# A top-1 expert layer computed densely, against one that first sorts the rows by expert through DRAM and then computes 88 tiles of one expert each

## What is computed

```python
router_logits = xf @ Wr + br                      # [10000, 8]
topk_logits, topk_idx = jax.lax.top_k(router_logits, TOP_K)      # TOP_K = 1
topk_gates = jax.nn.softmax(topk_logits, axis=1)
for k in range(TOP_K):
    idx_k = topk_idx[:, k]
    gate_k = topk_gates[:, k:k + 1]
    for e in range(E):                            # E = 8
        h = jax.nn.relu(xf @ W1[e] + b1[e])       # 512 -> 64
        oe = h @ W2[e] + b2[e]                    # 64 -> 512
        mask = (idx_k == e)[:, None]
        out = out + jnp.where(mask, gate_k * oe, 0.0)
...
x = x + _L0_ffn_ref(_layernorm(x, axis=-1)[None], ...)[0]
```

## Time and profile before

| | us |
|---|---|
| median of 3 runs | 2736.06 (2735.32 to 2736.74) |
| the profiled execution | 2733.61 |
| its span in the trace | 2731.8 |
| `nodes`, first PE work to the wait before `hidden` | about 10 to 1010 |
| `hidden` | about 1018 to 1487 |
| `mix` | about 1487 to 2132 |
| `ffn` | 2132 to 2732 |

### The profile page before, as it was taken

One profiled execution on the slowest core, in us unless ns is written; L12 is line 12 of the kernel. 1 busy time (PEld: TensorE's weight loads), 2 busy tenths in 40 slices (PEclk: granted clock), 3 DMA queues, 4 the chain that ended last, 5 costly groups with the idle time before them and its releaser, 6 DMA issues.

```text
span 2731.8 us, 36032 instructions
## 1 busy us (share of the span) xinstructions
PE 2612.9 (96%) x11712; PEld 2081.5 (76%) x11712; DVE 1836.8 (67%) x3708; ACT 1031.0 (38%) x1805; POOL 1061.6 (39%) x1009
## 2 busy tenths in 40 slices
PE   5999999999999989999999788999999899999999
PEld 4788888888888868888886556677777677777777
DVE  5577777777778744444443677788886677777774
ACT  3455454444444434443443232233332132232232
POOL 5677766666666620000000455555554111111110
PEclk9999999999999999999999899999999999999999
DMA  9767665555555554444444478787887332232231
GB/s 367 246 174 201 174 194 145 146 139 135 145 125 157 126 156 180 189 172 185 185 185 162 147 192 224 217 241 220 233 227 179 145 139 93 94 137 93 105 125 46
DMA packets 134566, 460.66 MB, mean 169 GB/s; under 512 B 26649, under 2 KB 27161, under 8 KB 99137
## 3 DMA queue, kind: packets, MB, share of 16 engines
q1 hardware_dynamic: 98624, 375.21, 37.6%
q0 software_dynamic: 35840, 84.23, 17.0%
HBM read 240.62 MB, written 218.76 MB: 168 GB/s over the span
## 4 chain that ended last, share of the span: by engine, by line
PE 82%; DMA 7%; DVE 5%; SPq 2%; issue 2%; ACT 2%; POOL 1%; POOLq 0%; DVEq 0%; ACTq 0%
PE bank L1206 63%; PE bank L1257 8%; DMA agg_d<-O,eidx 5%; PE bank L1213 3%; PE bank L1321 2%; DVE x2T_low L314 2%; PE bank L1421 1%; PE bank L417 1%; PE bank L418 1%; SPq L484 1%; DVE f_relu L1125 1%; PE bank L1332 1%; ACT f_relu L884 1%; SPq L486 1%; PE bank L1406 1%
## 5 line engine op out<-in xcount | busy, mean ns | idle before, releaser
L378 POOL DMA_INDIRECT agg_d<-O,eidx x160 | 275.4, 1721 | 234.6 <-DMA agg_d<-O,eidx 165.7
L314 POOL TENSOR_TENSOR G_low<-G,G_high 128x512 fp32r<-128x512 f32 x160 | 244.0, 1525 | 209.0 <-ACT G_high L439 209.0
L361 POOL DMA_INDIRECT G<-y_d,esrc x80 | 87.2, 1090 | 529.8 <-DMA y_d<-b_y 516.9
L397 DVE SCALAR_TENSOR_TENSOR Sj<-erow,dstf,tri 128x128 f32<-128x128 int32 x160 | 188.7, 1179 | 55.4 <-DMA agg_d<-O,eidx 55.3
L720 POOL TENSOR_SCALAR veps<-mv 128x1 f32<-128x1 f32 x80 | 26.5, 332 | 487.2 <-DVE mv L1098 487.2
L439 ACT CAST G_high<-G 128x512 fp32r<-128x512 f32 x160 | 99.2, 620 | 198.5 <-DVE G L958 175.4
L406 DVE SCALAR_TENSOR_TENSOR eidx<-cnt,todump,dstf 128x1 int32<-128x1 f32 x160 | 139.7, 873 | 7.6
L685 POOL TENSOR_TENSOR pd<-pd,low 128x512 f32<-128x512 f32 (+1 forms) x80 | 143.2, 1790 | 0.0
L314 POOL TENSOR_TENSOR a_xn_rows_low<-a_x,a_xn_rows_high 128x512 fp32r<-128x512 f32 x80 | 142.7, 1783 | 0.2 <-ACT a_xn_rows_high L749 0.2
L850 ACT CAST qz_high<-low 128x512 fp32r<-128x512 f32 x80 | 49.6, 620 | 239.4 <-PE bank L1206 152.5
L1206 PE MATMUL bank<-Wk_high,xnT_high 128*128 128x512 f32 x320 | 127.9, 400 | 6.3 <-DVE xnT_low L314 6.3
...
## 6 DMA issues: line engine op xcount, KB each, us to landing
...
q_d<-q_rows SPq DMA_DIRECT2D x80, 256.0 KB, 2.4
r_d<-r_rows SPq DMA_DIRECT2D x80, 256.0 KB, 3.8
...
```

The source lines that it names most:

```text
L314: return eng.tensor_tensor(out_, full, high.bitcast(F32), ALU.subtract)
L361: pool.indirect_dma_start(G[:, j, :], None, table, bass.IndirectOffsetOnAxis(ap=esrc[:, b, j:j + 1], axis=0)).then_inc(e_g[j], 16)
L378: pool.indirect_dma_start(agg, bass.IndirectOffsetOnAxis(ap=eidx[:, j, 0:1], axis=0), O[:, j, 0:width], None, compute_op=ALU.add).then_inc ...
L397: dve.scalar_tensor_tensor(Sj[:, :], row, dstf[:, b, j:j + 1], tri[:, :], ALU.is_equal, ALU.mult, accum_out=cnt[:, j:j + 1]).then_inc(e_cn ...
```

## The change

`nodes`, the fold, `hidden` and `mix` stay as they are, but for semaphores that are merged and for preparations of the last stage: POOL's clearing at t = 10 of `mix` goes away, two copies on ACT and two subtractions on DVE go away, and SP loads other constants (a table of 573 KB, later the weights' halves). In their place `ffn` becomes two passes with a hinge between them.

**`route`**, 20 groups: x2 and its statistics as before, now into `rows` with 8 extra words for each row (mean, 1/sqrt, -mean/sqrt, gate, row number). ACT makes the normalised rows, PE turns them, ACT evacuates them unsplit, and PE computes the logits by fp32 matmuls with 8 moving columns (4 for each tile), row form. DVE finds the maximum and the one-hot without an index instruction; PE ranks the rows inside the group by matmuls with a lower-triangular and an all-ones matrix (8 matmuls), DVE adds the running count of each expert, and POOL scatters the rows (2080 bytes each) to their place in `xs_d`, an area for each expert.

**The hinge**: DVE computes from the eight counts, by 19 instructions each waiting for the one before, two tables of 88 entries: the expert of a tile and its first row. SP writes a padding tile of 128 rows behind the last row of each expert (8 DMAs at an address read from SBUF into a register) and waits for the scatters.

**`expert`**, 88 tiles of 128 rows of one expert (80 full tiles, and at most one broken tile for each expert): SP reads the tile's first row from the table and loads it; ACT normalises; PE turns (4); ACT and DVE evacuate as halves; PE computes the hidden layer of the one expert, 4 matmuls of 128 and 4 of 64 columns, with weights at an address read from the table; DVE adds the bias; PE turns the hidden row block (1), ACT and DVE apply relu and split; PE makes the output by 2 matmuls of 512 columns; DVE computes the row number and x2 + gate * output; POOL scatters the tile to its rows of `out`.

The core of the diff:

```diff
-                if isinstance(t, int) and t == 10:
-                    pool.tensor_scalar(expand[:, :, :].rearrange("p c n -> p (c n)"),
...
-                    for b in range(2):
-                        pool.tensor_scalar(maskT[:, b, :], trash[:, 0:1].to_broadcast([P, GROUP]), 0.0, None,
-                                           ALU.mult).then_inc(s_zf, 1)
...
+                    need(sp, r_x2, 13 * (g - 3) - 2)
+                    sp.dma_start(rp[k][:, :, :].rearrange("p j n -> p (j n)"), part_d[g]).then_inc(r_in[k], 16)
+                    sp.dma_start(ra[k][:, :, :].rearrange("p j n -> p (j n)"), agg2_g[g]).then_inc(r_in[k], 16)
...
+            sp.wait_ge(r_tb, 1)
+            for e in range(EXP):
+                end = sp.value_load(runi[0:1, e:e + 1], min_val=0, max_val=EXP * REG - P)
+                sp.dma_start(xs_d[bass.ds(end, P), :], pad_in).then_inc(r_pad, 16)
...
+            sp.wait_ge(r_tb, TB)
+
+            def expert(turn, k):
+                s = 8 * turn + k
+                need(sp, x_o, s - 7)
+                row = sp.value_load(tabS[0:1, bass.ds(s, 1)], min_val=0, max_val=EXP * REG - P)
+                sp.dma_start(xs[:, k, :], xs_d[bass.ds(row, P), :]).then_inc(x_in[k], 16)
...
         @block.gpsimd
...
+                if active(g, 3, NG):
+                    k3 = (k - 3) % 4
+                    need_apart(pool, r_ch, CH * (g - 2))
+                    for j in range(TG):
+                        pool.indirect_dma_start(xs_d.ap(), bass.IndirectOffsetOnAxis(ap=place[:, k3, j, 0:1], axis=0),
+                                                rows[:, k3, j, :], None).then_inc(r_sc[k3], 16)
...
+                if active(s, 5, XT):
+                    i4 = (k - 5) % 4
+                    need_apart(pool, x_o, s - 4)
+                    pool.indirect_dma_start(out, bass.IndirectOffsetOnAxis(ap=xid[:, i4, 0:1], axis=0),
+                                            xo[:, i4, :], None).then_inc(x_sc[i4], 16)
...
         @block.scalar
...
+                if active(s, 3, XT):
+                    act.wait_ge(x_ht, s - 2)
+                    need(act, x_y, s - 4)
+                    act.activation(xh[:, 1 - b, 0, :], bank[5 - b][:, 0:P], ACT.Relu)
+                    act.activation(xh[0:EH, 1 - b, 1, :], bank[5 - b][0:EH, 0:P], ACT.Relu).then_inc(x_r, 1)
+                if active(s, 0, XT):
+                    act.wait_ge(x_in[k], 16 * (turn + 1))
+                    need(act, x_tr, s - 1)
+                    act.activation(xn[:, b, :], xs[:, k, 0:D], ACT.Identity, bias=xs[:, k, D + 2:D + 3],
+                                   scale=xs[:, k, D + 1:D + 2]).then_inc(x_xn, 1)
+                if active(s, 1, XT):
+                    act.wait_ge(x_tr, s)
+                    need(act, x_h, s - 2)
+                    act.copy(xT_[0][:, 1 - b, :, :], chunks(bank[1 - b])).then_inc(x_ev, 1)
...
         @block.vector
...
+                def best():
+                    dve.wait_ge(r_l, 4 * (g - 1))
+                    dve.tensor_tensor(lg[:, :, :], bank[2 + 4 * (k % 2)][:, 0:TG * EXP].rearrange(
+                        "p (j e) -> p j e", j=TG), each(brs), ALU.add).then_inc(r_ch, 1)
...
+                    dve.wait_ge(r_ch, n + 5)
+                    dve.tensor_reduce(m2[:, :], sc[:, :, :], axis=mybir.AxisListType.X, op=ALU.max).then_inc(r_ch, 1)
+                    dve.wait_ge(r_ch, n + 6)
+                    dve.tensor_tensor(onehot[:, :, :], over(m2), each(rev), ALU.is_equal).then_inc(r_ch, 1)
...
+                    dve.wait_ge(r_rk, g - 1)
+                    dve.tensor_tensor(pos[:, :, :], bank[3][:, 0:TG * EXP].rearrange("p (j e) -> p j e", j=TG),
+                                      each(run), ALU.add).then_inc(r_ch, 1)
...
+                x2(0)
+                x2(1)
+                if active(g, 2, NG):
+                    best()
+                x2(2)
+                if active(g, 2, NG):
+                    places()
+                x2(3)
+            quad_turns(dve, route, 2)
...
+            dve.wait_ge(r_ch, CH * NG)
+            made(1, dve.tensor_copy(runi[one, :], run[one, :]))
...
+            made(18, dve.tensor_copy(tabE[one, :], tabf[one, 0, :]))
+            made(19, dve.tensor_scalar(tabS[one, :], tabf[one, 1, :], run[one, EXP - 1:EXP], None, ALU.min))
...
+                if active(s, 3, XT):
+                    dve.wait_ge(x_r, s - 2)
+                    low = xh[EH:P, 1 - b, 0, :]
+                    dve.scalar_tensor_tensor(low, bank[5 - b][EH:P, 0:P], 0.0, low.bitcast(F32), ALU.max,
+                                             ALU.subtract).then_inc(x_rl, 1)
+                if active(s, 2, XT):
+                    turn2, k2 = lagged(turn, k, 2)
+                    e = dve.value_load(tabE[0:1, bass.ds(8 * turn2 + k2, 1)], min_val=0, max_val=EXP - 1)
+                    dve.wait_ge(x_h, s - 1)
+                    dve.tensor_tensor(xt1[:, b, :], bank[2 + b][:, EH:P],
+                                      b1s[:, bass.ds(e, 1), :].rearrange("p a h -> p (a h)"), ALU.add
+                                      ).then_inc(x_hs, 1)
+                    need(dve, x_ht, s - 3)
+                    dve.wait_ge(x_hs, 2 * (s - 2) + 1)
+                    dve.tensor_tensor(xhs[:, b, :].rearrange("p (a h) -> p a h", a=2),
+                                      bank[2 + b][:, None, 0:EH].to_broadcast([P, 2, EH]),
+                                      xt1[:, b, None, :].to_broadcast([P, 2, EH]), ALU.add).then_inc(x_hs, 1)
+                if active(s, 4, XT):
+                    turn4, k4 = lagged(turn, k, 4)
+                    dve.wait_ge(x_y, s - 3)
+                    if not (isinstance(s, int) and s < 8):
+                        turn8, k8 = lagged(turn, k, 8)
+                        dve.wait_ge(x_sc[k % 4], 16 * (2 * turn8 + k8 // 4 + 1))
+                    dve.scalar_tensor_tensor(xid[:, k % 4, :], order[:, bass.ds(8 * turn4 + k4, 1)],
+                                             xs[:, k4, D + 5:D + 6], xs[:, k4, D + 4:D + 5], ALU.mult, ALU.add)
+                    dve.scalar_tensor_tensor(xo[:, k % 4, :], bank[6 + b][:, :], xs[:, k4, D + 3:D + 4],
+                                             xs[:, k4, 0:D], ALU.mult, ALU.add).then_inc(x_o, 1)
+                if active(s, 1, XT):
+                    dve.wait_ge(x_ev, s)
+                    low_half(dve, xT_[1][:, 1 - b, :, :], chunks(bank[1 - b]), xT_[0][:, 1 - b, :, :]
+                             ).then_inc(x_lo, 1)
...
         @block.tensor
...
+                def rank():
+                    pe.wait_ge(r_ch, CH * (g - 2) + 7)
+                    chosen = onehot[:, :, :].rearrange("p j e -> p (j e)")
+                    pe.matmul(bank[3][:, 0:TG * EXP], before[:, :], chosen, start=True, stop=False)
...
                 if active(g, 1, NG):
+                    turn_row(0)
+                    turn_row(1)
+                    logits(0)
+                    turn_row(2)
+                if active(g, 2, NG):
+                    rank()
+                if active(g, 1, NG):
+                    logits(1)
+                    turn_row(3)
+                    logits(2)
+                    logits(3)
...
+                if active(s, 3, XT):
+                    pe.wait_ge(x_hs, 2 * (s - 2))
+                    need(pe, x_rl, s - 4)
+                    pe.transpose(bank[5 - b][:, 0:P], xhs[:, 1 - b, :], ident[:, :]).then_inc(x_ht, 1)
...
+                    e = pe.value_load(tabE[0:1, bass.ds(8 * turn2 + k2, 1)], min_val=0, max_val=EXP - 1)
+                    pe.wait_ge(x_lo, s - 1)
+                    need(pe, x_hs, 2 * (s - 3))
                     for c in range(KC):
+                        pe.matmul(bank[2 + b][:, 0:2 * EH], xT_[0][:, b, c, :],
+                                  W1x[:, bass.ds(e, 1), c, :, :].rearrange("p a n h -> p (a n h)"),
+                                  start=c == 0, stop=False)
...
+                        last = pe.matmul(bank[2 + b][:, 0:EH], xT_[1][:, b, c, :],
+                                         W1x[:, bass.ds(e, 1), c, 0, :].rearrange("p a h -> p (a h)"),
+                                         start=False, stop=c == KC - 1)
+                    last.then_inc(x_h, 1)
+                if active(s, 1, XT):
+                    pe.wait_ge(x_xn, s)
+                    need(pe, x_lo, s - 2)
+                    turn_tile(bank[1 - b], xn[:, 1 - b, :]).then_inc(x_tr, 1)
+                if active(s, 4, XT):
+                    turn4, k4 = lagged(turn, k, 4)
+                    e = pe.value_load(tabE[0:1, bass.ds(8 * turn4 + k4, 1)], min_val=0, max_val=EXP - 1)
+                    pe.wait_ge(x_rl, s - 3)
+                    need(pe, x_o, s - 5)
+                    pe.matmul(bank[6 + b][:, :], xh[:, b, 0, :],
+                              W2a[:, bass.ds(e, 1), :].rearrange("p a n -> p (a n)"), start=True, stop=False)
+                    pe.matmul(bank[6 + b][:, :], xh[0:HD + 2, b, 1, :],
```

(2 more changed lines are left out.)

611 lines of the change are left out of this document (312 added, 299 removed).

## The result

The changed kernel takes 2905.35 us (median of 4 runs, 2902.22 to 2920.30) against 2735.69 us for the kernel before (4 runs): a ratio of 1.063, with a 95% interval of 1.061 to 1.065. It is slower, as forecast, but by 170 us and not by 49, and outside the range of 2708 to 2880. The profiled execution has a span of 2901.5 us.

A forecast was written before the change was run, and what follows sets the result against it. Serial hand-offs between engines, not PE's work, were taken to bound it: routing to 2345, hinge to 2378, then 8.5 + 377.2 (84 rounds at 4.49) + 10 + 7 to 2781, forecast 2785 us, range 2708 to 2880.

The forecast's parts named there:

- a serial loop: In `expert`, DVE's low half, PE's hidden layer, turn and output matmuls, then DVE's output set the pace, 4.49 us a tile.
- the clock: PE's steps in `route` and `expert` were priced without a clock fall, small matmuls at 0.12 to 0.23 us.
- The clock rival: PE's clock falls to 1.2 GHz in the last stage: round 5.4 us, some 15 us more in routing, 2876; chance 0.18.
- The register load: In `expert`, ahead of PE's output matmuls: 0.56 us plus 0.10 for instructions around it, bounds 0 and 1.3.
- 4.49: Round of one `expert` tile in us, the sum of the loop's steps on PE and DVE; bounds 3.7 and 5.9.
- The fast rival: In `expert`, register load fetched while PE works and small matmuls at 0.12 us: round 3.69 us, total 2718; chance 0.22.
- 11.2 us a group: Period of one group in `route`, from DVE's 10.5 and DMA's 9.1 to 13.1 us; bounds 10 and 13.
- its wait for the rank: In `route`, PE finishes the rank 0.6 to 1.4 us after DVE wants it; taken as 1 us.
- the ring through POOL's scales: In `route`, POOL's four small steps of at most 0.57 us each, with the scatters under 9 us, counted as hidden.
- The rival that DMA binds `route`: DMA transfers set the `route` period, 18 groups at 13.1 instead of 11.2 us: +34, 2819; chance 0.13.
- The hinge: Between `route` and `expert`: serial piece 15.6 us, SP's padding tiles 12, first tile's load 1.0 + 3.8; sum 33 us.
- The clearing: POOL's clearing at the start of `mix`, removed: at most 4.3 us come back, taken as -4.

The follow-up runs named there:

- e3: Changed kernel with DVE's low half ahead of bias step and output, and PE's turn ahead of the hidden layer, in `expert`: 2772.91 us.
- e4: Changed kernel with one move in `expert`: DVE's low half ahead of the output, PE's order untouched: 2809.39 us.
- e16: e9 with one move on DVE in `route`, a group's fourth x2 ahead of the placing of the group two back: 2710.14 us.
- e2: Changed kernel with 4 unused matmuls of 512 columns added on PE for each tile of `expert` only: 2785.84 us.
- e1: Changed kernel with unused 512-column matmuls: 44 ahead of `route`, 8 a group in it, 70 in the hinge, 4 a tile in `expert`: 2829.44 us.
- e13: e9 with unused matmuls of 512 columns added, 44 between `mix` and `route` and 16 in each group of `route`: 2715.48 us.
- e14: e13 with only the first of four chunks in the router's logits, so another choice of experts: 2701.69 us.
- after: The changed kernel as it stands, in its profiled execution: 2905.35 us measured, span 2901.5 us.
- e9: e5 with DVE's register load at the start of its step, ACT's copy ahead of normalising, 3 unused matmuls a tile, not 4: 2724.02 us.
- e5: Changed kernel with both moves of e3 and the 4 unused matmuls a tile of e2, `route` untouched: 2742.59 us.

## Why the prediction was wrong

**The direction and its reason were right.** PE's amount of work was not the question; a serial loop, DVE's low half to hidden layer to turn to output matmuls to DVE, sets the round. Its two cuts, e3 and e4, came within 2.1 us of what the loop's arithmetic gives.

**The step that failed is the clock.** The forecast let PE keep it and gave the fall a chance of 0.18. Its sum took PE's steps of a round as 1.2 + 0.48 + 0.62 = 2.30 us and a small matmul of `route` as 0.12 us. The clock fell as `route` began and never rose; the steps took 1.91 + 0.93 + 0.87 = 3.71 us and a small matmul 0.212 (100 us for 471 records in e16). e2 shows that it is the clock: with it at 1.00 the same steps took 2.27 us and the whole 120 us less. Why the clock stays at 0.50 under this work, even with PE busy for 100 of 100 us (e3, e16), and rises when unused matmuls of 512 columns are added, no run here shows.

The clock rival's own round, 5.4 us, is the measured one (5.39), and by its own mechanism: PE's part about 3.8, the register load hidden. Its total of 2876 was still 29 us short: 19 in `route` and hinge (264 us by its sum, 283.2 measured) and 17 in `expert` (479 against 495.8, where the first `x_out` came 16.1 us after the first `x_xn` and 87 rounds followed, instead of 8.5 us and 84), less 6.5 at the start of the stage. For `route` and hinge it priced the fall at 15 us, where PE's small matmuls alone are 11.9 us a group and a ring with 6.2 us of PE work goes around at 12.5.

What spoke for the fall stood in the earlier trace rows: the clock at 0.54 after PE had waited for the start of the stage. It was read as an effect of long gaps, with the stretch beside it, PE busy for 1.77 of 4 us at 1.00, taken as the typical one. But that one was from the start of the program, and no row of before showed what the clock does under several hundred microseconds of work of 8 and 128 columns. The section of the Trainium skill that the prediction named, of TensorE: Matmul & The Clock Gate, speaks of a clock that oscillates; the rows after show no oscillation but 0.50 in each stretch from 2132 to 2900 us. With unused matmuls in `route` it changed between the levels (e1, e13 and e14).

**The register load was put on the path, and it isn't there.** The forecast held that PE's sequencer can't run far ahead, and added 0.56 + 0.10 us. The sequencer does run ahead: load and register work take 0.58 us beside the hidden layer, no gap is seen in `after`, and 0.24 us in e9, where nothing else is late. e2 measures what the forecast meant by 4.49: 3.99 us. Of PE's terms the rest holds: hidden layer 1.12 (forecast 1.2), turn 0.49 (0.48), output matmuls 0.66 (0.62). DVE's part with its semaphores was 1.76 us in `after`, from the end of L1601 at 2608.11 to PE's next start at 2609.87, where the forecast had 0.04 + 1.49. The two errors pull opposite ways: with the load rightly left out, the forecast would have missed by more.

**The fast rival had the load right.** "Fetched while PE still works" is what the trace shows. Its 3.69 us and its total of 2718 are refuted by e2 (3.99 with the clock up), since the hidden layer took 1.12 and not 0.96 and DVE's part was longer; rounds under 3.69 came only after the order was changed (e5 on).

**That the forecast's 11.2 us a group lies near e13's 11.07 is an accident.** e13 has full clock, but 1.04 us of its ring are unused matmuls, and no run shows the changed kernel's `route` at full clock without them. DVE's sum was right (9.3 us), but its wait for the rank was 3.1 us at half clock and 1.7 in e13, not 1, and it comes from the ring through POOL's scales, which the forecast had as hidden. Those four steps were priced at up to 0.57 us each; the power took 1.04, and together they are 2.5 us of latency. The scatters were cheaper than thought, 0.97 us of POOL and not 1.55 to 1.64. The rival that DMA binds `route` is out: at a period of 10.5 us the DMA share is 0.86, so a group's transfers take 9.0 us, just under the forecast's 9.1 to 13.1.

**The hinge** was 38.1 us, not 33. From the last x2 to the last placing it took 19.3 instead of 15.6, with PE at half clock. The pads came next with 15.4 us until SP went on, instead of 12: eight pads took 11.1 us from the first issue to the end of the last, where 8.0 was assumed. The first row load took 3.4 us to the first `x_xn`, instead of 4.8.

**The clearing** measured about 8 us and not 4, but the runs don't tell the two apart.

The sum of it, by the profiled execution: `route` + 29, hinge + 5, `expert` + 93, start of the stage - 6, together 121, which is the distance from 2785 to 2905. In `expert` the clock is worth about + 120 (e2), so by itself it is as large as the whole error.
